# Two layers of attention scores on one core: value matmuls moved behind the first score matmul of a step, row maxima of the second layer taken from two PSUM banks by one instruction

## The chip, the cores and the metric

One core of a Trainium2 chip runs the whole kernel. The metric is the device time of one execution in microseconds (us); lower is better.

## The reference

The input x is (4, 1024, 128), with 16 heads of 8 channels. Cut to what matters here:

```
# layer 1
h      = layernorm(x)
q,k,v  = h @ Wq + bq, h @ Wk + bk, h @ Wv + bv          # (4, 16, 1024, 8)
s      = q @ k.T * 8**-0.5 + slope[h] * (i - j)          # causal: -inf above the diagonal
x      = x + layernorm(softmax(s) @ v @ Wo + bo)
# layer 2
h      = layernorm(x)
a      = softmax(q @ k.T / sqrt(8)) @ v @ Wo + bo        # not causal, no slope
u      = h + layernorm(a) * g1 + b1
x      = x + layernorm(u + layernorm(moe(u)) * g2 + b2)  # 8 experts, 2 chosen per token
```

So there are 4 x 16 score matrices of 1024 x 1024 per layer, causal in the first layer and full in the second, and each needs its row maxima before the exponentials.

## The kernel before

**Slots and steps.** The function `attend` goes through 32 slots, 16 per layer; a slot is four heads (`GH`) of one batch. `program()` writes one list of steps by hand, and each engine runs through this same list and does its own part of it, in that order. The kinds of step that matter:

- `a`: scores with queries on the partitions, only to find row maxima. TensorE writes a chunk of up to 512 columns into a PSUM bank (L388; on the causal diagonal two mask matmuls follow, L393) and VectorE takes the maximum of each row (`tensor_reduce`, L589). The a steps of a slot run one and two slots ahead of its exponentials.
- `m`: VectorE joins and splits the maxima (L598, L601, L603), after the last a of a slot. `mtr`: TensorE transposes them (L399) into a bank, VectorE copies that out (L609), and SyncE puts it into rows of the query operand `fq` by DMA.
- `b`: scores with keys on the partitions and the maxima already subtracted. TensorE writes 128x512 into one of three banks (`B_BANKS`, L411), ScalarE takes the exponential into `probs` (L474). The k-th b waits until the exponential of b number k-3 is done. Four b's, one per head, make a quad.
- `pv`: value matmuls of one quad, four heads by column groups, all into one bank (L424). `oev`: ScalarE reads this bank out at the end of half a slot (L479).
- Row steps: the work on token rows between the layers, spread over the slots by `row_steps()`: `project` (L433), `turn` (L439), `values_mm` (L443), `q` and `k` (L233 to L235), `logits` and `rank` on TensorE, each written into one bank that VectorE reads out (`y`, `turned`, `values`, `q_out`, `k_out`, `gate`, `pos`); GpSimd and SyncE do the rest.

**The inner loop.** A slot of the second layer has 16 inner steps, one of the first has 12. In inner step i the order is: the first b of quad i+3, half of the a's, the second b, the other a's, the last two b's, then `m` or `mtr` where they are due, then pv of quad i+1 (and `oev`), then the row steps. In the second layer 64 a's of one head and 512 columns fall on 16 inner steps, so about four on each (five in one of them, three in that of `mtr`). `m` is due in inner step 8 of 16 and `mtr` in step 9, behind its a's; in the first layer in steps 4 and 5 of 12.

**The ring of banks.** a, `mtr` and the TensorE row steps take the four banks `a_bank` in turn, each step one bank; `bank_free` makes TensorE wait for the reader of the step that is four places back in this ring.

**Which rows of the array.** A score matmul contracts 64 partitions, two heads, and so works in the lower or the upper half of the array (`rows_`, by head // 2). b runs through heads 0, 2, 1, 3 (`B_HEADS`), a too.

TensorE's, VectorE's, ScalarE's and GpSimd's waits are all on counts in program order, so an instruction that waits holds everything behind it on its engine.

Of the kernel before, what the change touches and what calls it, by code (L numbers as in the profile page):

```python
# [19 lines left out]
F32 = mybir.dt.float32  # L20
# [6 lines left out]
P = 128  # L27
# [13 lines left out]
HALF = 512  # L41
# [10 lines left out]
    return [start * start ** i for i in range(H)]  # L52


A_BANKS = 4
B_BANKS = 3
PROBS = 4
LOADS = 16 * 3 * GH
# [16 lines left out]
class Plan:  # L75


    def __init__(self, causal):
        self.causal = causal

        self.chunks = []
        for qt in range(TB):
            for kh in range(2):
                n = min(HALF, (qt + 1) * P - kh * HALF) if causal else HALF
                if n <= 0:
                    continue
                per = 2 if n <= HALF // 2 else 1
                for j in (0, 2) if per == 2 else (0, 2, 1, 3):
                    self.chunks.append((qt, kh, list(range(j, j + per)), n))

# [12 lines left out]
        self.mt_step = self.a_steps  # L103


PLANS = (Plan(True), Plan(False))


def plan_of(s):
    return PLANS[s // S]  # L110
# [62 lines left out]
def program():  # L173
# [10 lines left out]
    for s in range(SLOTS):  # L184
        p = plan_of(s)
        if s + 3 < SLOTS:
            out.append(("load", s + 3, 0))
        if s + 1 < SLOTS:
            out.append(("stage", s + 1, 0))
        weights = [4 - (i == p.mt_step) - .5 * (i == p.m_step) for i in range(p.nq)]  # L190
        for i in range(p.nq):
            early = i < p.a_steps
            part = range(p.a_steps) if early else range(p.a_steps, p.nq)
            target = s + 1 if early else s + 2
            ass = []
# [24 lines left out]

# [17 lines left out]
def attend(nc, loaded, query, key, rests, tokens, sums, by_head, dens, inverses, inverse_rows, ident, half_ident,  # L238
# [3 lines left out]
    with ExitStack() as ctx:  # L242
# [6 lines left out]
        def bank(name):  # L249
            return ctx.enter_context(nc.psum_tensor(f"at_{name}", [P, HALF], F32))  # L250
# [8 lines left out]
        a_bank = [bank(f"a{i}") for i in range(A_BANKS)]  # L259
        b_bank = [bank(f"b{i}") for i in range(B_BANKS)]  # L260
        pv_bank = bank("pv")

# [27 lines left out]
        for what, s, n in steps:  # L290
# [6 lines left out]
        ring = [step for step in steps if step[0] in RING]  # L297
        place = {step: k for k, step in enumerate(ring)}
# [10 lines left out]
        def done(eng, semaphore, kind, s, n, per=1):  # L309

            if (s, n) in number.get(kind, {}):
                eng.wait_ge(semaphore, per * number[kind][s, n])
# [20 lines left out]
            return qh, kt, q0, (qh + 1) * HALF - q0  # L333

        def bank_of(step):
            return a_bank[place[step] % A_BANKS]

        def block_of(x, n):
            return x[:, n * HQ:(n + 1) * HQ, :]
# [16 lines left out]
        def _(pe):  # L356
            def bank_free(step):

                if place[step] < A_BANKS:
                    return  # L360
                what, s, n = ring[place[step] - A_BANKS]
                if what == "a":
                    done(pe, a_read, "a", s, n)
                elif what == "mtr":
                    done(pe, m_read, "mtr", s, n)
                else:
                    reader = dict(project="y", turn="turned", values_mm="values", q="q_out", k="k_out", logits="gate",
                                  rank="pos")[what]
                    after(pe, reader, n)

            for step in steps:
                what, s, n = step
# [3 lines left out]
                if what == "a":  # L376
# [7 lines left out]
                    k = len(heads)  # L384
                    scores = misc[:, 0:k * w].rearrange("p (k w) -> p k w", k=k)
                    rows_ = slice(PAIR * (heads[0] // 2), PAIR * (heads[0] // 2 + 1))
                    first = heads[0] % 2
                    mm = pe.matmul(scores, fq[g][rows_, qt * P:(qt + 1) * P],  # L388
                                   km[g][rows_, first:first + k, kh * HALF:kh * HALF + w],
                                   start=True, stop=not diagonal)  # L390
                    if diagonal:
                        for i in range(2):
                            mm = pe.matmul(scores[:, :, w - P:w], half_ident[rows_, i, :],  # L393
                                           half_mask[rows_, i, None, :].broadcast_to([PAIR, k, P]),
                                           start=False, stop=(i == 1))
# [90 lines left out]
        def _(dve):  # L486
# [91 lines left out]
            for step in steps:  # L578
                what, s, n = step
                if what == "a":  # L580
                    qt, kh, heads, w = plan_of(s).chunks[n]
                    done(dve, a_made, "a", s, n)
                    if n == 0:
                        if s == 0:
                            dve.wait_ge(init, 5)
                        if s >= 1:
                            dve.wait_ge(m_step, 2 * s - 1)
                    k = len(heads)
                    dve.tensor_reduce(mx[:, kh, qt, heads[0]:heads[0] + k],  # L589
                                      bank_of(step)[:, 0:k * w].rearrange("p (k w) -> p k w", k=k),  # L590
                                      AX.X, ALU.max).then_inc(a_read, 1)
# [1289 lines left out]
```

## Time and profile before

| | |
|---|---|
| time, median of 3 runs | 1684.19 us (1681.83 to 1684.7) |
| profiled execution | 1682.8 us, span 1681.1 us |
| TensorE matmul busy | 1424.7 us (85%) |
| VectorE busy | 1296.1 us (77%) |
| ScalarE busy | 1097.2 us (65%) |
| GpSimd busy | 536.7 us (32%) |
| mean granted TensorE clock | 0.915 of full speed |

The span is time from the first to the last instruction. TensorE matmuls are pipelined, so that its busy share says little about how near it is to its peak. Slots of the first layer end at about 618 us in the trace, those of the second at 1352 us; behind that lies the expert part, which the change doesn't touch.

### The profile page before, as it was taken

The page shows a single profiled execution, that of the slowest core. Times are in us where ns is not written, and L with a number is a line of the kernel's source. Part 1 is how long each engine was busy: PE and PEld are TensorE (multiplying, and loading weights), DVE is VectorE, ACT ScalarE, POOL GpSimd, SP SyncE. Part 2 cuts the span into 40 slices and gives each one's busy share as a digit, 9 for nine tenths or more (in the row PEclk, how much of TensorE's full clock was granted, in tenths as well). Part 3 has the DMA queues.
Part 4 walks back from the last instruction along what each step waited for, and adds up shares of the span by engine and source line. Part 5 has one row for each costly group of instructions (what it writes and reads, how often), then busy time and mean ns, then how long its engine had stood idle before and what let it go on. Part 6 is the DMA issues. An engine that isn't in the chain of part 4 may idle for free. (4 is left out here: it accounts for less than half of the span.)

```text
span 1681.1 us, 27511 instructions
## 1 busy us (share of the span) xinstructions
PE 1424.7 (85%) x9143; PEld 712.0 (42%) x9143; DVE 1296.1 (77%) x2638; ACT 1097.2 (65%) x2256; POOL 536.7 (32%) x624
## 2 busy tenths in 40 slices
PE   3389999999999999999999999999999831999400
PEld 3145555555555443443344333433343221788300
DVE  4378888889888989999999999999998023655355
ACT  4036677677676557778777787778777820999444
POOL 5114544534525322340122312323141406000274
PEclk9569999999999989999999999999999965999855
DMA  6402241322322222133221122102210124788322
GB/s 168 145 28 73 84 133 50 112 81 65 102 89 72 74 71 66 43 90 91 69 65 53 52 64 78 54 32 75 61 46 33 57 78 131 224 247 248 110 63 69
DMA packets 105822, 148.96 MB, mean 89 GB/s; under 512 B 13236, under 2 KB 63164, under 8 KB 105680
## 3 DMA queue, kind: packets, MB, share of 16 engines
q1 hardware_dynamic: 100348, 138.18, 28.0%
q0 software_dynamic: 4096, 8.40, 1.7%
q8 instruction: 73, 1.20, 0.3%
q10 hardware_dynamic: 1236, 0.62, 0.2%
q14 instruction: 69, 0.57, 0.1%
HBM read 78.70 MB, written 67.13 MB: 87 GB/s over the span
## 5 line engine op out<-in xcount | busy, mean ns | idle before, releaser
L474 ACT ACTIVATE at_probs<-at_b 128x512 f32<-128x512 f32 (+3 forms) x1792 | 866.3, 557 | 380.8 <-PE at_b L411 376.2
L589 DVE TENSOR_REDUCE at_mx<-at_a 128x1 f32<-128x512 f32 (+3 forms) x1664 | 992.0, 661 | 89.5 <-PE at_a L393 28.3
L411 PE MATMUL at_b<-fq,km 64*128 64x512 f32 (+3 forms) x1792 | 669.1, 439 | 16.7 <-ACT at_probs L474 13.3
L388 PE MATMUL at_a<-km,fq 64*128 64x512 f32 (+2 forms) x1664 | 549.9, 453 | 46.3 <-DMA fq<-rest 35.2
L411 PEld LDWEIGHTS at_b<-fq,km 64*128 64x128 f32 x1792 | 295.9, 187 | 405.0 <-ACT at_probs L474 340.5
L424 PE MATMUL at_pv<-at_probs,at_vst 128*32 128x512 f32 (+3 forms) x3584 | 442.0, 566 | 0.0
L388 PEld LDWEIGHTS at_a<-km,fq 64*128 64x128 f32 x1664 | 273.8, 191 | 146.2 <-DVE at_mx L589 82.9
L747 POOL TENSOR_SCALAR_AFFINE_SELECT at_probs<-at_probs 128x512 f32<-128x512 f32 x128 | 81.5, 636 | 284.0 <-ACT at_probs L474 283.1
L1653 POOL DMA_INDIRECT t_got<-expert_out,t_out_pos x64 | 63.5, 993 | 171.4 <-issue 171.4
L424 PEld LDWEIGHTS at_pv<-at_probs,at_vst 128*32 128x32 f32 x3584 | 71.0, 108 | 104.2 <-issue 49.2
L393 PE MATMUL at_a<-half_mask,half_ident 64*128 64x128 bf16 (+1 forms) x768 | 108.7, 251 | 0.0
L1566 DVE TENSOR_TENSOR t_hid_lo<-t_hid,t_hid_hi 128x512 fp32r<-128x512 f32 x92 | 61.3, 686 | 60.5 <-ACT t_hid_hi L1419 60.5
L1414 ACT ACTIVATE t_hid<-t_bank_h,t_bias 128x512 f32<-128x512 f32 x92 | 63.0, 687 | 2.7 <-PE t_bank_h L235 2.6
L752 POOL DMA_INDIRECT expert_rows<-kept_u,route_pos x48 | 46.7, 974 | 36.5 <-DVE route_pos L873 23.5
L1419 ACT ACTIVATE t_hid_hi<-t_hid 128x512 fp32r<-128x512 f32 x92 | 55.5, 635 | 0.0
L393 PEld LDWEIGHTS at_a<-half_mask,half_ident 64*128 64x128 bf16 x768 | 43.2, 100 | 25.6 <-issue 17.4
L1577 DVE SCALAR_TENSOR_TENSOR t_z<-t_got,route_weight,t_weighed 128x128 f32<-128x128 f32 x32 | 9.1, 346 | 47.4 <-ACT t_weighed L1428 47.4
L637 POOL TENSOR_TENSOR at_rstd<-at_mean_var,pow_cols 128x4 f32<-128x4 f32 x26 | 5.3, 203 | 124.9 <-DVE at_mean_var L501 124.9
L479 ACT ACTIVATE at_osb<-at_pv 128x512 f32<-128x512 f32 x64 | 39.4, 615 | 6.2 <-PE at_pv L424 1.9
L741 POOL COPY at_vst<-tokens 128x256 f32<-128x256 f32 x32 | 12.7, 397 | 95.3 <-PE at_pv L424 95.0
L637 POOL TENSOR_TENSOR at_turned_hi<-at_t,pow_cols 128x512 fp32r<-128x512 f32 x18 | 18.7, 1041 | 69.4 <-DVE at_t L532 69.4
L233 PE MATMUL t_bank_h<-t_x_t_hi,t_w 128*128 128x512 f32 x92 | 37.0, 402 | 3.1 <-issue 1.6
(237 smaller groups left out, 1254.2 us busy)
## 6 DMA issues: line engine op xcount, KB each, us to landing
t_w<-w_parts SPq DMA_DIRECT2D x46, 512.0 KB, 4.4
sums<-at_osb SPq DMA_DIRECT2D x64, 256.0 KB, 2.0
fq<-query SPq DMA_DIRECT2D x128, 96.0 KB
km<-key SPq DMA_DIRECT2D x128, 96.0 KB
w_parts<-at_parts SPq DMA_DIRECT2D x16, 512.0 KB, 3.0
query<-at_q_hi SPq DMA_DIRECT2D x24, 256.0 KB, 3.1
key<-at_k_hi SPq DMA_DIRECT2D x24, 256.0 KB, 3.7
t_x_tok<-expert_rows SPq DMA_DIRECT2D x23, 256.0 KB, 4.8
```

Of the source, the lines that this page charges most:

```text
L388: mm = pe.matmul(scores, fq[g][rows_, qt * P:(qt + 1) * P], km[g][rows_, first:first + k, kh * HALF:kh * HALF + w], start=True, stop=not d ...
L393: mm = pe.matmul(scores[:, :, w - P:w], half_ident[rows_, i, :], half_mask[rows_, i, None, :].broadcast_to([PAIR, k, P]), start=False, sto ...
L411: pe.matmul(b_bank[k % B_BANKS][:, 0:w], km[g][rows_, j % 2, kt * P:(kt + 1) * P], fq[g][rows_, q0:q0 + w], start=True, stop=True).then_in ...
L424: mm = pe.matmul(pv_bank[HW * j:HW * (j + 1), HALF - w:HALF], vst[s % 2][:, kt, j, :], probs[n % PROBS][:, j, 0:w], start=(kt == 0), stop= ...
L474: act.activation(probs[t % PROBS][:, j, 0:w], b_bank[k % B_BANKS][:, 0:w], ACT.Exp).then_inc(exp_done, 1)
L589: dve.tensor_reduce(mx[:, kh, qt, heads[0]:heads[0] + k], bank_of(step)[:, 0:k * w].rearrange("p (k w) -> p k w", k=k), AX.X, ALU.max).the ...
L747: pool.affine_select(block_, block_, [[0, GH], [1, P]], ALU.is_ge, 0.0, base=0, channel_multiplier=-1).then_inc(masked, 1)
L752: pool.indirect_dma_start(out=xs[:, :], out_offset=bass.IndirectOffsetOnAxis(ap=routing["pos"][:, k, t:t + 1], axis=0), in_=kept_u[:, t, : ...
L1414: op = act.activation(hid[:, f, :], h_bank[f][:, :], ACT.Gelu, bias=bias[:, n, f:f + 1])
L1419: op = act.activation(hid_hi[i][:, f, :], hid[:, f, :], ACT.Identity)
L1566: op = dve.tensor_tensor(hid_lo[i][:, f, :], hid[:, f, :], hid_hi[i][:, f, :].bitcast(F32), ALU.subtract)
L1653: pool.indirect_dma_start(out=got[i][:, k, t, :], out_offset=None, in_=ys[:, :], in_offset=bass.IndirectOffsetOnAxis(ap=out_pos[:, k, n * ...
```

## The change

1. In `program()` pv of quad i+1 and its `oev` come right behind the first b of inner step i; `m`, `mtr` and the row steps stay at the end of the step. The a's now lie between the second, third and fourth b.
2. In the second layer a chunk is a pair of heads, (0, 2) or (1, 3), in two neighbouring banks. TensorE writes both (in the other order in every second chunk, so that the array halves alternate), then one `tensor_reduce` of 128 x 2 x 512 reads both. A slot has 32 such chunks in place of 64, two in each inner step.
3. The ring now counts places: a pair must start at an even place, so behind a single bank's use one place is skipped. `bank_free` waits for the last users of all places that a step takes.

```diff
-                for j in (0, 2) if per == 2 else (0, 2, 1, 3):
-                    self.chunks.append((qt, kh, list(range(j, j + per)), n))
+                if paired:
+                    self.chunks += [(qt, kh, (tuple(range(j, j + per)), tuple(range(j + 2, j + 2 + per))), n)
+                                    for j in range(0, 2, per)]
...
-PLANS = (Plan(True), Plan(False))
+PLANS = (Plan(True, False), Plan(False, True))
...
-            out += bs[:1] + ass[:half] + bs[1:2] + ass[half:] + bs[2:]
+            out += bs[:1]
+            at, q = (s, i + 1) if i + 1 < p.nq else (s + 1, 0)
+            if at < SLOTS:
+                out.append(("pv", at, q))
+                if q in plan_of(at).half_end:
+                    out.append(("oev", at, plan_of(at).half_end.index(q)))
+            out += bs[1:2] + ass[:half] + bs[2:3] + ass[half:] + bs[3:]
             if s + 1 < SLOTS:
                 if i == p.m_step:
                     out.append(("m", s + 1, 0))
                 if i == p.mt_step:
                     out.append(("mtr", s + 1, 0))
-            at, q = (s, i + 1) if i + 1 < p.nq else (s + 1, 0)
-            if at < SLOTS:
-                out.append(("pv", at, q))
-                if q in plan_of(at).half_end:
-                    out.append(("oev", at, plan_of(at).half_end.index(q)))
             out += rows.get((s, i), [])
...
+        place, users_before, users = {}, {}, [None] * (2 * A_PAIRS)
+        spot = 0
+        for step in steps:
+            if step[0] in RING:
+                width = len(plan_of(step[1]).chunks[step[2]][2]) if step[0] == "a" else 1
+                spot += spot % width
+                place[step] = spot % len(users)
+                taken = range(place[step], place[step] + width)
+                users_before[step] = [u for k, u in enumerate(users) if k in taken and u is not None]
+                for k in taken:
+                    users[k] = step
+                spot += width
...
-                if place[step] < A_BANKS:
-                    return
-                what, s, n = ring[place[step] - A_BANKS]
-                if what == "a":
-                    done(pe, a_read, "a", s, n)
+                for what, s, n in users_before[step]:
+                    if what == "a":
+                        done(pe, a_read, "a", s, n)
...
+                    parts = list(enumerate(heads))
+                    for at, js in parts[::-1] if n % 2 else parts:
+                        k = len(js)
+                        bank_ = misc if len(heads) == 1 else pair_with(step)[:, at, :]
...
+                    elif k == 1:
+                        dve.tensor_reduce(mx[:, kh, qt, j:j + 3:2], pair_with(step)[:, :, 0:w], AX.X,
+                                          ALU.max).then_inc(a_read, 1)
```

## Rows read from the trace of the kernel before

**Rows 1.** Windows: span, busy us (instructions) of PE, PEld, DVE, ACT, POOL, clock, DMA.
```profile
300.00:400.00 100.00, 98.76 (x809) 51.63 (x805) 86.29 (x178) 71.02 (x164) 43.54 (x56) 1.00 0.31 93
570.00:618.00 48.00, 45.76 (x228) 20.34 (x229) 43.33 (x82) 22.51 (x51) 15.12 (x19) 0.86 0.12 30
1100.00:1200.00 100.00, 98.34 (x587) 38.14 (x590) 95.64 (x176) 78.43 (x153) 22.91 (x31) 1.00 0.21 65
1320.00:1345.00 25.00, 20.67 (x119) 6.00 (x111) 0.00 (x0) 20.05 (x40) 11.50 (x12) 1.00 0.17 61
```

**Rows 2.** Waits from 800 to 1300 us: total, times, longest.
```profile
PEld at_b L411 <- ACT at_probs L474: 166.7, 276, 1.7
```

**Rows 3.** Timeline, last slot, where no a is left: start, length, engine, instructions.
```profile
1323.21 0.73 PE L411 MATMUL at_b<-fq,km 64*128 64x512 f32 x3
1323.74 2.07 ACT L474 ACTIVATE at_probs<-at_b 128x512 f32<-128x512 f32 x4 [0.53 <-PE at_b L411]
1324.39 0.49 PE L411 MATMUL at_b<-fq,km 64*128 64x512 f32 x1 [0.45 <-ACT at_probs L474]
1324.81 1.06 PE L424 MATMUL at_pv<-at_probs,at_vst 128*32 128x512 f32 x8
1325.81 0.73 PE L411 MATMUL at_b<-fq,km 64*128 64x512 f32 x3
```

**Rows 4.** Timeline, second layer with its a's, three stretches.
```profile
1002.38 0.50 PE L411 MATMUL at_b<-fq,km 64*128 64x512 f32 x1
...
1003.56 0.18 PEld L411 LDWEIGHTS at_b<-fq,km 64*128 64x128 f32 x1 [0.29 <-ACT at_probs L474]
...
1004.98 0.50 PE L411 MATMUL at_b<-fq,km 64*128 64x512 f32 x1
...
1006.40 7.36 DVE L589 TENSOR_REDUCE at_mx<-at_a 128x1 f32<-128x512 f32 x12
...
1013.21 0.50 PE L411 MATMUL at_b<-fq,km 64*128 64x512 f32 x1
...
1013.98 2.48 DVE L589 TENSOR_REDUCE at_mx<-at_a 128x1 f32<-128x512 f32 x4 [0.21 <-PE at_a L388]
```

**Rows 5.** Groups by form, 60 to 700 us: busy us, mean ns, idle before.
```profile
L589 DVE TENSOR_REDUCE at_mx<-at_a 128x1 f32<-128x512 f32 x579 | 359.7, 680 | 27.1 <-PE at_a L393 14.0 <-PE at_a L388 11.2
...
L589 DVE TENSOR_REDUCE at_mx<-at_a 128x1 f32<-128x384 f32 x128 | 64.2, 548 | 10.4 <-PE at_a L393 10.2
```

**Rows 6.** Timeline, logits with a project behind pv, and a turn behind pv.
```profile
1061.16 0.27 PE L233 MATMUL at_a<-gw_hi,at_turned_hi 128*128 128x8 f32 x1
...
1063.59 0.50 PE L411 MATMUL at_b<-fq,km 64*128 64x512 f32 x1
...
1086.19 0.66 PE L439 MATMUL at_a<-ident,kept_u 128*128 128x128 f32 x4
1086.78 0.49 PE L411 MATMUL at_b<-fq,km 64*128 64x512 f32 x1
```

**Rows 7.** Timeline, an inner step with mtr, from its first b.
```profile
1066.19 0.50 PE L411 MATMUL at_b<-fq,km 64*128 64x512 f32 x1
...
1066.87 0.19 DVE L598 TENSOR_TENSOR at_mfull<-at_mx 128x32 f32<-128x32 f32 x1
...
1067.32 0.21 DVE L603 TENSOR_TENSOR at_m_parts<-at_mfull,at_m_parts 128x32 fp32r<-128x32 f32 x1
...
1067.81 0.33 PE L399 MATMUL at_a<-ident,at_m_parts 128*128 128x128 f32 x1
...
1068.07 1.06 PE L424 MATMUL at_pv<-at_probs,at_vst 128*32 128x512 f32 x8
```

**Rows 8.** Timeline, the value matmuls around the step with five a's.
```profile
1074.32 1.06 PE L424 MATMUL at_pv<-at_probs,at_vst 128*32 128x512 f32 x8
...
1077.29 1.07 PE L424 MATMUL at_pv<-at_probs,at_vst 128*32 128x512 f32 x8
```

More of the change, by code:

```diff
@@ L52, in slopes @@
     return [start * start ** i for i in range(H)]
-A_BANKS = 4
+A_PAIRS = 2
 B_BANKS = 3
@@ L75, with __init__ @@
 class Plan:
-    def __init__(self, causal):
+    def __init__(self, causal, paired):
         self.causal = causal
@@ L87, in __init__ @@
                 per = 2 if n <= HALF // 2 else 1
-                for j in (0, 2) if per == 2 else (0, 2, 1, 3):
-                    self.chunks.append((qt, kh, list(range(j, j + per)), n))
+                if paired:
+                    self.chunks += [(qt, kh, (tuple(range(j, j + per)), tuple(range(j + 2, j + 2 + per))), n)
+                                    for j in range(0, 2, per)]
+                else:
+                    self.chunks += [(qt, kh, (tuple(range(j, j + per)),), n)
+                                    for j in ((0, 2) if per == 2 else (0, 2, 1, 3))]
         self.quads = []
@@ L258, in attend @@
         osb = sb("osb", [P, 2, HALF])
-        a_bank = [bank(f"a{i}") for i in range(A_BANKS)]
+        a_pair = [ctx.enter_context(nc.psum_tensor(f"at_a{i}", [P, 2, HALF], F32)) for i in range(A_PAIRS)]
         b_bank = [bank(f"b{i}") for i in range(B_BANKS)]
@@ L296, in attend @@
                 series[s, n] = len(series) + 1
-        ring = [step for step in steps if step[0] in RING]
-        place = {step: k for k, step in enumerate(ring)}
+        place, users_before, users = {}, {}, [None] * (2 * A_PAIRS)
[10 more added lines that the diff above has]
+                spot += width
         row_order = [(what,) + n for what, s, n in steps if what in ENGINE_OF]
@@ L335, in bank_of, with pair_with @@
         def bank_of(step):
-            return a_bank[place[step] % A_BANKS]
+            return pair_with(step)[:, place[step] % 2, :]
+        def pair_with(step):
+            return a_pair[place[step] // 2]
         def block_of(x, n):
@@ L357, in bank_free @@
             def bank_free(step):
-                if place[step] < A_BANKS:
-                    return
-                what, s, n = ring[place[step] - A_BANKS]
-                if what == "a":
-                    done(pe, a_read, "a", s, n)
[L364 to L369, printed above, removed]
+                for what, s, n in users_before[step]:
+                    if what == "a":
+                        done(pe, a_read, "a", s, n)
+                    elif what == "mtr":
+                        done(pe, m_read, "mtr", s, n)
+                    else:
+                        reader = dict(project="y", turn="turned", values_mm="values", q="q_out", k="k_out", logits="gate",
+                                      rank="pos")[what]
+                        after(pe, reader, n)
             for step in steps:
@@ L382, in _ @@
                     diagonal = plan_of(s).causal and kh * HALF + w == (qt + 1) * P
[L384 to L395, printed above, removed]
+                    parts = list(enumerate(heads))
+                    for at, js in parts[::-1] if n % 2 else parts:
+                        k = len(js)
+                        bank_ = misc if len(heads) == 1 else pair_with(step)[:, at, :]
+                        scores = bank_[:, 0:k * w].rearrange("p (k w) -> p k w", k=k)
+                        rows_ = slice(PAIR * (js[0] // 2), PAIR * (js[0] // 2 + 1))
+                        first = js[0] % 2
+                        mm = pe.matmul(scores, fq[g][rows_, qt * P:(qt + 1) * P],
+                                       km[g][rows_, first:first + k, kh * HALF:kh * HALF + w],
+                                       start=True, stop=not diagonal)
+                        if diagonal:
+                            for i in range(2):
+                                mm = pe.matmul(scores[:, :, w - P:w], half_ident[rows_, i, :],
+                                               half_mask[rows_, i, None, :].broadcast_to([PAIR, k, P]),
+                                               start=False, stop=(i == 1))
                     mm.then_inc(a_made, 1)
@@ L587, in _ @@
                             dve.wait_ge(m_step, 2 * s - 1)
[L588 to L591, printed above, removed]
+                    k, j = len(heads[0]), heads[0][0]
+                    if len(heads) == 1:
+                        dve.tensor_reduce(mx[:, kh, qt, j:j + k],
+                                          bank_of(step)[:, 0:k * w].rearrange("p (k w) -> p k w", k=k),
+                                          AX.X, ALU.max).then_inc(a_read, 1)
+                    elif k == 1:
+                        dve.tensor_reduce(mx[:, kh, qt, j:j + 3:2], pair_with(step)[:, :, 0:w], AX.X,
+                                          ALU.max).then_inc(a_read, 1)
+                    else:
+                        dve.tensor_reduce(mx[:, kh, qt, :].rearrange("p (h k) -> p h k", k=k),
+                                          pair_with(step)[:, :, 0:k * w].rearrange("p h (k w) -> p h k w", k=k), AX.X,
+                                          ALU.max).then_inc(a_read, 1)
                 elif what == "m":
```

## Prediction, made before the changed kernel was run

> **What bounds the kernel now.** I read the windows first [rows 1]. In the second layer TensorE shows 98 us of work in 100, VectorE 96, ScalarE 78. That looks as if VectorE, next to full, set the pace. The last of these windows contradicts it: there no a is left, VectorE does nothing, and yet, as the timeline shows, the loop has not become faster. So I looked for the period of the inner step.
>
> In the last slot the first b of a step starts at 1323.21 and that of the next at 1325.81: 2.60 us [rows 3]. With four a's and their reductions the same distance is 1004.98 - 1002.38 = 2.60 us [rows 4]. Taking away the whole of VectorE's work changes nothing, so it is not the bound of an ordinary step. What is, can be followed in the same rows: first b at 1323.21; ScalarE starts on it at 1323.74 (0.53 later); the fourth b must have the bank of the first and starts at 1324.39, 1.18 behind the first, after an exponential of some 0.6 and a semaphore's delay; the value matmuls start 0.42 later, at 1324.81; and the next first b is 1.00 behind them. 0.53 + 0.65 + 0.42 + 1.00 = 2.60. In the chain of waits the same wait is the largest, 166.7 us in 500 [rows 2]. With a's running, TensorE is held for only 0.29 us of a step at that place [rows 4], because the a's fill the rest; still it is held.
>
> The second thing that a step can be held by is VectorE's backlog. Four reductions take 4 x 0.607 = 2.43 us when they run without a gap (12 in 7.36 us: 7.36 less one length of 0.68, by 11 [rows 4, 5]), so 0.17 us of a step is spare, and where VectorE has other work it lags and TensorE waits for a bank.
>
> **Part 1, the order of b and pv.** Written as a line, the new order looks different. The loop is a cycle, though, and I start both at pv:
>
> before: pv, b, a's, b, a's, b, b, pv
> after: pv, b, a's, b, a's, b, b, pv
>
> They are the same. Only the names have moved: the b behind pv used to be the first of its quad and is now the second. B_BANKS is 3 in both, so the fourth b of a burst still waits for the exponential of the first one of that burst, and pv stands behind it. The chain is 2.60 us as before. I take this part at 0 for an ordinary step; the chance that it does release the chain is a rival below. pv of a quad now runs one burst earlier with respect to its exponentials and, in the first layer, to GpSimd's diagonal masks. Almost a full cycle is left between them; I take 0. `oev` stands between the same instructions of ScalarE's cycle as before: 0. Behind an earlier pv the buffer of probabilities comes free earlier, and nothing waits for it.
>
> What does move in the cycle are `mtr` and TensorE's row steps. Before, a row step stood behind pv, and `mtr` between the fourth b and pv. Now both stand between the third b and the fourth, so the fourth b and pv queue behind them, and what they wait for counts in full.
>
> **Part 2, one reduction for two banks.** The trace has no reduction of 1024 columns. From 384 to 512 columns it goes from 548 to 680 ns [rows 5], 1.03 ns a column, so one of 1024 should take 0.68 + 0.53 = 1.21 us, and without a gap 1.21 - 0.07 = 1.14 against 2 x 0.607 = 1.21 for two. A pair saves 0.07, and 512 pairs save 38 us of VectorE's time. The lower bound is no saving, the upper one 2 x 0.68 - 1.21 = 0.15 a pair, if instructions didn't overlap at all.
>
> The Trainium skill (VectorE: DVE Perf Modes, The DRAIN you can't avoid) says that the next instruction does not start until the pipe is empty. By that rule a pair saves the 0.15; the trace differs, since 12 reductions of 0.68 us fit in 7.36 us, and the measurement decides.
>
> Little of the 38 us can come out of the time, because an ordinary step isn't VectorE's. What can: the inner step with five a's takes 1077.29 - 1074.32 = 2.97 us [rows 8] and becomes one of two pairs, -0.37, in about 12 slots (this row stands for them): -4. In the stretch 570 to 618 us the first layer's last slot has 64 a's of the second layer in 12 inner steps and VectorE is at 43 of 48 us [rows 1]; there 32 pairs save 2.4 us. Backlogs behind the statistics and the routing work shrink a little: -3. Together -9; bounds 0 and -20.
>
> **Part 3, the ring.** This is where I expect the loss. In an inner step of the second layer the pairs X and Y now fill all four banks. A single use at the end of the step (`mtr` or a row step) takes the first bank of X, and TensorE must wait until VectorE has read all of X. Before, it waited for the use four places back, an a that was long read.
>
> When is X read? Count from the b behind pv. The reduction of the first a's starts 1013.98 - 1013.21 = 0.77 later [rows 4], and that is about when both a's of X are there. So X is read from 0.77 to 1.98, and a single can start at 2.03 with a semaphore's 0.05. Then the fourth b follows, which on an ordinary step starts at 1.18.
>
> *Row steps in the second layer.* A turn behind pv costs its own time, 1086.78 - 1086.19 = 0.59, and logits with project 1063.59 - 1061.16 = 2.43 [rows 6]. That remains. On top of it comes 2.03 - 1.18 = 0.85, since the fourth b starts that much later than it otherwise would. By the tables of row steps such a place occurs 26 times while pairs are running (10 from the last rows of the first layer, 16 for the second's three batches, the logits and project of one step sharing a pair). 26 x 0.85 = 22. Bounds: 0 if X was read in time, 1.2 each (31) if VectorE lags by 0.35 more.
>
> *mtr in the second layer.* m starts at 1066.87, 0.68 behind the first b, ends at about 1067.53 (1.34), and `mtr` runs at 1067.81 (1.62), pv at 1068.07, 1.88 behind the b where 1.60 is usual: it costs 0.28 now [rows 7]. In the new order X of this step stands behind m on VectorE and ahead of `mtr` on TensorE, by the same rule. So `mtr` waits for m and then for 1.21 us of X: reductions end about 0.13 sooner, m ends at 1.20, X is read until 2.42, `mtr` starts at 2.47, the fourth b 0.27 later at 2.74, against 1.18: it costs 1.56. That is +1.28 in each of 16 slots (those whose a's belong to the second layer at that time): +20. Bounds 0.9 and 1.8 each, 14 to 29. What waits behind: b, pv, and through them ScalarE, which has nothing to do for over a microsecond, and VectorE after Y.
>
> *First layer.* The a's are single and the ring as before. A row step there costs one change of array shape more, since the sequence b, row step, b, pv has one more than b, pv, row step, b. The third b is through by about 0.9 (the fourth's 0.29 of waiting ends at 1.18 [rows 4]) and a change of shape takes 0.42 (from b to pv [rows 3]), so a row step starts at about 1.3, where the fourth b wants to start at 1.18: +0.12, and more where VectorE lags, as it often does there (86 of 100 us [rows 1]). I take 0.2 for 46 row steps, +9, and 0.13 for 14 `mtr`, +2; bounds 0 and 30.
>
> The Trainium skill (TensorEngine Tiling (Array Packing), Key Properties) has it that changing the tiling mode drains TensorE. The trace agrees so far: 0.42 us from a lone b to pv. By the rule alone the first layer would be put at 46 x 0.12 = 6 us.
>
> **Sum.** +22 + 20 + 11 - 9 = +44 us. On the profiled execution's 1682.8 this is 1727; the median lies 1.4 above that, so 1729.
>
> **Rivals.** (a) *VectorE was the pace after all*, and the pairs free it: 512 x 0.07 = 38 us less, 1646. For it: 96 of 100 us busy. Against: 2.60 us without any reduction. It decides only if most steps wait for banks rather than for the exponential. By the skill's page on VectorE it would be 512 x 0.15 = 75 us, 1609; I give this 0.02 of the chance.
> (b) *The new order breaks the chain*: the wait of 0.29 us in a step goes, 256 x 0.29 = 74 us, 1610. For it: pv could cover the exponential. Against: the cycle above, with the fourth b ahead of pv in both.
> (c) *The singles' wait is hidden*, because VectorE is ahead: then parts 2 and 3 leave +2 to +11 - 9, that is 1680 to 1690. Against: X can't be read before it is written, 0.77 behind the burst's start.
> (d) *The waits add up with lag*: upper bounds, 31 + 29 + 30 - 5 = +85, 1769.
>
> **Chances.** Forecast (slower by some 17 to 68) 0.66; (d) 0.08; (c) 0.12; (a) and (b) 0.14 together. A difference of 0.2%, 3.4 us, is about what a measurement of this kernel can tell from none. Of (c) I count 0.04 within it, 0.06 slower and 0.02 faster: slower 0.66 + 0.08 + 0.06 = 0.80, same 0.04, faster 0.02 + 0.14 = 0.16. For 8 times in 10 the range is 1690 to 1752; it leaves out (a), (b) and the end of (d). If the forecast's mechanism holds, its own range is 1701 to 1752.
>
> **What the profile after should show.** The period of an ordinary step still 2.60 us, with the fourth b held by the exponential of the first of its burst. Reductions of 128x2 from 1024 columns of 1.21 us, 512 of them, and VectorE's idle time larger, not smaller. TensorE waiting for the reduction (L589's successor) ahead of `mtr` and the row steps of the second layer, about 40 times at 0.8 to 1.3 us. Steps with `mtr` at 4.1 to 4.2 us, with a turn at 4.0. The first layer's length within 20 us of what it was. Wrong would be: an ordinary step clearly under 2.60 (then the cycle argument fails), or singles that start at once (then part 3 fails).

## The result, and the profile after

The changed kernel takes 1728.6 us (median of 4 runs, 1724.93 to 1733.97) against 1683.4 for the kernel before beside it (4 runs): 1.0271 times as long, 95% interval 1.0242 to 1.0301. The forecast was 1729 (1690 to 1752). Its profiled execution took 1724.93 us, with a span of 1723.2 us and a mean granted clock of 0.908.

The windows come first again; the columns are those of [rows 1]. From the second on, the stretches lie later than those of before, as the kernel itself does, and the second is longer.

```profile
300.00:400.00 100.00, 97.47 (x800) 49.62 (x797) 84.49 (x170) 70.28 (x162) 42.34 (x55) 1.00 0.32 96
575.00:640.00 65.00, 52.76 (x310) 23.11 (x308) 53.04 (x59) 31.80 (x72) 21.42 (x26) 0.84 0.22 67
1110.00:1210.00 100.00, 95.01 (x550) 35.57 (x550) 83.06 (x96) 70.29 (x136) 26.46 (x34) 0.93 0.19 55
1360.00:1385.00 25.00, 20.38 (x114) 6.13 (x112) 0.00 (x0) 20.06 (x40) 13.97 (x15) 1.00 0.18 66
```

In the second layer VectorE went from 96 us in 100 to 83, and ScalarE, whose work is the same, from 78 to 70. The second number says that the stretch got slower; the first, that VectorE's amount of work does not set its pace: it has more idle time than before. TensorE can still wait for a single reduction, and the timelines below show that it does. In the last slot, where no a is left, 25 us hold the same 40 exponentials as before. The profile's page, in its groups of instructions over the whole span, shows VectorE's cheaper work (name, form, count, then busy us, mean ns, idle before):

```profile
L613 DVE TENSOR_REDUCE at_mx<-at_a 128x2 f32<-128x1024 f32 x512 | 600.0, 1217 | 109.6 <-PE at_a L407 109.4
L609 DVE TENSOR_REDUCE at_mx<-at_a 128x1 f32<-128x512 f32 (+3 forms) x640 | 359.6, 628 | 101.2 <-PE at_a L412 44.6
```

A pair is 1217 ns long; the estimate was 1.21 us.

**Where the time went.** `oev`, the read-out of the value bank, marks the end of each slot. Slots are counted from 0, so slot 15 is the first layer's last.

| us | before | after | change | my terms |
|---|---|---|---|---|
| slots 0 to 14, ends at | 570.2 | 581.5 | +11.3 | +11 |
| slot 15 | 48.1 | 52.7 | +4.6 | -2.4 |
| second layer, 16 slots | 732.9 | 760.4 | +27.5 | +22 +20 -6.6 |
| behind it, to the span's end | 329.9 | 328.6 | -1.3 | 0 |
| span | 1681.1 | 1723.2 | +42.1 | +44 |

In the text below a single is a use of one bank by `mtr` or a row step, and X is the first pair of an inner step.

**An ordinary step** of the changed kernel, one without a single, in the timeline:

```profile
1008.47 0.49 PE L430 MATMUL at_b<-fq,km 64*128 64x512 f32 x1
...
1009.10 0.21 PEld L407 LDWEIGHTS at_a<-km,fq 64*128 64x128 f32 x2 [0.34 <-DVE at_mx L613]
...
1009.24 2.36 DVE L613 TENSOR_REDUCE at_mx<-at_a 128x2 f32<-128x1024 f32 x2 [0.25 <-PE at_a L407]
...
1009.65 0.18 PEld L430 LDWEIGHTS at_b<-fq,km 64*128 64x128 f32 x1 [0.25 <-ACT at_probs L493]
...
1010.07 1.07 PE L443 MATMUL at_pv<-at_probs,at_vst 128*32 128x512 f32 x8
1011.07 0.50 PE L430 MATMUL at_b<-fq,km 64*128 64x512 f32 x1
```

From the b behind pv to the next one: 1011.07 - 1008.47 = 2.60 us. The last b of the burst starts 1.18 behind the first, released by the exponential, pv 0.42 later, the next b 1.00 later. These are the three terms of [rows 3]. New is that VectorE is idle for 0.25 us of the step and that an a waits 0.34 for the reduction of the pair ahead. Neither lengthens the step.

**The step with `mtr`**:

```profile
1001.77 0.50 PE L430 MATMUL at_b<-fq,km 64*128 64x512 f32 x1
...
1002.33 0.19 DVE L625 TENSOR_TENSOR at_mfull<-at_mx 128x32 f32<-128x32 f32 x1
...
1002.91 2.35 DVE L613 TENSOR_REDUCE at_mx<-at_a 128x2 f32<-128x1024 f32 x2
...
1004.18 0.33 PE L418 MATMUL at_a<-ident,at_m_parts 128*128 128x128 f32 x1 [1.04 <-DVE at_mx L613]
1004.44 0.50 PE L430 MATMUL at_b<-fq,km 64*128 64x512 f32 x1
1004.87 1.06 PE L443 MATMUL at_pv<-at_probs,at_vst 128*32 128x512 f32 x8
1004.97 0.60 ACT L493 ACTIVATE at_probs<-at_b 128x512 f32<-128x512 f32 x1 [1.09 <-PE at_b L430]
1005.86 0.50 PE L430 MATMUL at_b<-fq,km 64*128 64x512 f32 x1
```

m is short (0.19), but VectorE then reads pair X from 1002.91, and `mtr` wants X's first bank. The trace names the reduction as releaser, 1.04 us. `mtr` starts 2.41 behind the first b, the last b 2.67 and pv 3.10; the prediction had 2.47 and 2.74. ScalarE meanwhile stands idle for 1.09 us. The step takes 1005.86 - 1001.77 = 4.09 us.

That is the undisturbed step. In five of the second layer's 15 steps with `mtr` VectorE has other work between m and X, and the step takes 4.7 to 5.25 us. In three of them it is the statistics of a row step:

```profile
1096.32 0.19 DVE L625 TENSOR_TENSOR at_mfull<-at_mx 128x32 f32<-128x32 f32 x1
...
1096.90 0.86 DVE L517 BATCH_NORM_STATS2 at_stats<-at_y 128x6 f32<-128x128 f32 x4
...
1098.09 2.32 DVE L613 TENSOR_REDUCE at_mx<-at_a 128x2 f32<-128x1024 f32 x2
...
1099.34 0.33 PE L418 MATMUL at_a<-ident,at_m_parts 128*128 128x128 f32 x1 [2.21 <-DVE at_mx L613]
```

X is read from 1098.09 here, some 1.2 us later, and `mtr` waits 2.21 in place of 1.04. With single banks in the same order (e1 below) the steps that hold nothing but `mtr` all take 2.93 to 2.95 us. So a pair makes `mtr` pay for what else VectorE does ahead of it.

**The step with a turn**:

```profile
1115.37 0.50 PE L430 MATMUL at_b<-fq,km 64*128 64x512 f32 x1
...
1116.14 2.36 DVE L613 TENSOR_REDUCE at_mx<-at_a 128x2 f32<-128x1024 f32 x2 [0.35 <-PE at_a L407]
...
1117.42 0.66 PE L458 MATMUL at_a<-ident,kept_u 128*128 128x128 f32 x4 [0.79 <-DVE at_mx L613]
1118.01 0.50 PE L430 MATMUL at_b<-fq,km 64*128 64x512 f32 x1
1118.44 1.06 PE L443 MATMUL at_pv<-at_probs,at_vst 128*32 128x512 f32 x8
```

X is read from 0.77 behind the first b (predicted 0.77), the turn starts at 2.05 (2.03). The waits from 640 to 1395 us count how often this happens (total, times, longest):

```profile
DVE at_mx L613 <- PE at_a L407: 98.0, 189, 3.5
...
PEld at_a L418 <- DVE at_mx L613: 26.2, 15, 2.6
...
PEld at_a L238 <- DVE at_mx L613: 9.4, 8, 1.3
...
PEld at_a L458 <- DVE at_mx L613: 9.2, 8, 1.2
...
PEld at_a L452 <- DVE at_mx L613: 5.6, 5, 1.1
```

L238 is the helper of q, k and logits, L458 the turn, L452 the project. With two more lines of two waits each (`values_mm` and rank) single uses of a bank wait for a pair's reduction 40 times. The first line says that in the same stretch VectorE waited 98 us for TensorE: what it saves turns into idle time.

**Account of the second layer.** I took every step from pv to pv, and added up what it lies over 2.60 us, by what it holds.

| steps, us over 2.60 each | before | after | change in all |
|---|---|---|---|
| turn (8) | 0.59 | 1.46 | +7.0 |
| project (5) | 1.49 | 1.96 | +2.3 |
| logits (3) | 1.44 | 2.50 | +3.2 |
| logits and project (3) | 2.43 | 3.30 | +2.6 |
| other row steps (8, then 7) | 0.91 | 1.49 | +3.1 |
| with `mtr` (15) | 0.80 | 1.81 | +15.2 |

That is +18 and +15, 33 in all. Added up in the same way, the steps without singles lie 27.5 us over before and 19.2 after, so 8 less. The 3 us that are then still missing to the slots' +27.5 are about one step, which the count has more after than before (254 and 253).

### The profile page after: what moved, and what is told of

Same layout as the page of the kernel before. It is cut to its first block and busy times, and to the rows that moved or that the text cites. A ratio compares the mean times of both kernels' runs of the same rounds, so it can differ in the third digit from the quotient of the medians.

```text
span 1723.2 us, 27495 instructions
## 1 busy us (share of the span) xinstructions
PE 1422.6 (83%) x9143; PEld 684.9 (40%) x9143; DVE 1255.3 (73%) x2126; ACT 1106.2 (64%) x2256; POOL 537.6 (31%) x624
## 5 line engine op out<-in xcount | busy, mean ns | idle before, releaser
L493 ACT ACTIVATE at_probs<-at_b 128x512 f32<-128x512 f32 (+3 forms) x1792 | 876.0, 556 | 416.1 <-PE at_b L430 410.3
L613 DVE TENSOR_REDUCE at_mx<-at_a 128x2 f32<-128x1024 f32 x512 | 600.0, 1217 | 109.6 <-PE at_a L407 109.4
L430 PE MATMUL at_b<-fq,km 64*128 64x512 f32 (+3 forms) x1792 | 658.5, 437 | 14.2 <-ACT at_probs L493 9.6
L407 PE MATMUL at_a<-km,fq 64*128 64x512 f32 (+2 forms) x1664 | 507.8, 463 | 53.4 <-DMA fq<-rest 35.9
L430 PEld LDWEIGHTS at_b<-fq,km 64*128 64x128 f32 x1792 | 299.6, 189 | 457.0 <-ACT at_probs L493 402.2
L443 PE MATMUL at_pv<-at_probs,at_vst 128*32 128x512 f32 (+3 forms) x3584 | 449.1, 574 | 0.4 <-ACT at_probs L493 0.4
L609 DVE TENSOR_REDUCE at_mx<-at_a 128x1 f32<-128x512 f32 (+3 forms) x640 | 359.6, 628 | 101.2 <-PE at_a L412 44.6
L407 PEld LDWEIGHTS at_a<-km,fq 64*128 64x128 f32 x1664 | 235.7, 192 | 151.0 <-DVE at_mx L613 84.0
```

The costliest lines, as they stand in the source:

```text
L407: mm = pe.matmul(scores, fq[g][rows_, qt * P:(qt + 1) * P], km[g][rows_, first:first + k, kh * HALF:kh * HALF + w], start=True, stop=not d ...
L430: pe.matmul(b_bank[k % B_BANKS][:, 0:w], km[g][rows_, j % 2, kt * P:(kt + 1) * P], fq[g][rows_, q0:q0 + w], start=True, stop=True).then_in ...
L443: mm = pe.matmul(pv_bank[HW * j:HW * (j + 1), HALF - w:HALF], vst[s % 2][:, kt, j, :], probs[n % PROBS][:, j, 0:w], start=(kt == 0), stop= ...
L493: act.activation(probs[t % PROBS][:, j, 0:w], b_bank[k % B_BANKS][:, 0:w], ACT.Exp).then_inc(exp_done, 1)
L609: dve.tensor_reduce(mx[:, kh, qt, j:j + k], bank_of(step)[:, 0:k * w].rearrange("p (k w) -> p k w", k=k), AX.X, ALU.max).then_inc(a_read, 1)
L613: dve.tensor_reduce(mx[:, kh, qt, j:j + 3:2], pair_with(step)[:, :, 0:w], AX.X, ALU.max).then_inc(a_read, 1)
```

## The experiments

Every kernel was timed beside the kernel before (1681.9 to 1682.7 us). Edits are against the changed kernel where nothing else is said.

### The parts by themselves

**e1_order**: the new order with single banks in the second layer too.

```diff
-PLANS = (Plan(True, False), Plan(False, True))
+PLANS = (Plan(True, False), Plan(False, False))
```

> The new order alone: pv behind the first b, but both layers with one a per bank and one reduction each. My theory (the cycle of b's and pv is the same, only mtr and the row steps have moved in front of the fourth b; the wait for a whole pair is what makes them dear in the second layer): ordinary steps 2.60 us, the first layer up to 582 us as in the changed kernel (570 before), mtr steps of the second layer at about 3.3 instead of 4.08, row steps there about 0.15 above before; in all 1683 + 11 + 6 + 4 = 1704 (1692 to 1712). Rival 1, the order is the whole loss: 1729. Rival 2, the pairs are the whole loss: 1683, and the first layer ends where it did before.

Measured: 1693.6 us, 1.0079 (1.0055 to 1.0103), less than expected but inside the range. Slots 0 to 14 end at 579.9, slot 15 takes 54.2, the second layer 726.8: 6 us less than before. So the first layer's whole loss comes from the order, and the second layer's is nothing that the order does alone. (The 6 us less are no gain of the order that is shown: in the kernel before, four steps are lengthened by some 7 us by a meeting that this kernel happens not to have; more on it below.) In the timeline `mtr` waits only for m here, and the last b follows 1.52 behind the first, in place of 2.67:

```profile
1077.05 0.49 PE L430 MATMUL at_b<-fq,km 64*128 64x512 f32 x1
...
1078.34 0.30 PE L418 MATMUL at_a<-ident,at_m_parts 128*128 128x128 f32 x1 [0.33 <-DVE at_m_parts L630]
1078.57 0.50 PE L430 MATMUL at_b<-fq,km 64*128 64x512 f32 x1
1078.99 1.07 PE L443 MATMUL at_pv<-at_probs,at_vst 128*32 128x512 f32 x8
```

**e2_pairs**: pairs with the old order. **e3_pairs_late**: the same, with `mtr` behind pv as well.

```diff
e2
-            out += bs[:1]
-            at, q = (s, i + 1) if i + 1 < p.nq else (s + 1, 0)
-            if at < SLOTS:
-                out.append(("pv", at, q))
...
-            out += bs[1:2] + ass[:half] + bs[2:3] + ass[half:] + bs[3:]
+            out += bs[:1] + ass[:half] + bs[1:2] + ass[half:] + bs[2:]
...
+            at, q = (s, i + 1) if i + 1 < p.nq else (s + 1, 0)
+            if at < SLOTS:
+                out.append(("pv", at, q))
...
             out += rows.get((s, i), [])
e3, against e2
-                if i == p.mt_step:
-                    out.append(("mtr", s + 1, 0))
...
+            if s + 1 < SLOTS and i == p.mt_step:
+                out.append(("mtr", s + 1, 0))
             out += rows.get((s, i), [])
```

> The pairs alone: the order of before (pv and the row steps behind the fourth b, mtr between the fourth b and pv). My theory: row steps find the pair read by the time pv is over and cost nothing more than before; mtr still waits for m and a reduction of 1024 columns, about 0.9 us in 16 slots = +14; the last slot of the first layer, where four pairs go through two places in a step, +4; steps with five a's gone, -4, backlogs -3: 1694 (1684 to 1702). Rival 1 (the order is the whole loss): 1683 or less. Rival 2 (the pairs are the whole loss): 1729. Rival 3 (fewer VectorE instructions pay): 1683 - 38 = 1645.

> As the pairs alone, but mtr is put behind pv, where it finds its bank read. My theory: the 14 us of e2_pairs go away, mtr steps at about 2.9 us: 1680 (1672 to 1690). Rival: if the wait ahead of mtr is hidden or is not for the pair, no difference to e2_pairs.

Measured: e2 1686.5 us, 1.0032 (1.0022 to 1.0043), inside its range but under the 1694 expected; e3 1678.9, 0.9975 (0.9963 to 0.9987), as expected. From e2 to e3 it gains 7.6 us, though, not the 14 that I had put on `mtr`'s wait: the shortest steps with `mtr` fell from 3.65 to 3.15 us, not to 2.9. The order alone costs 11 us, the pairs alone 4, both 46 (1.0271 of 1682): some 30 us belong to neither, only to their meeting. With pairs and the row steps behind pv the step with a turn takes 3.19 us as before, and one with a project 3.69, where single banks took 4.19: in such steps VectorE did lag, and pairs give 0.5 back.

**e5_mtr_late**: the kernel before, with `mtr` behind pv and nothing else. **e6_two_reduces**: e3, with each pair read by two reductions of 512.

```diff
-                        dve.tensor_reduce(mx[:, kh, qt, j:j + 3:2], pair_with(step)[:, :, 0:w], AX.X,
+                        dve.tensor_reduce(mx[:, kh, qt, j:j + 1], pair_with(step)[:, 0, 0:w], AX.X, ALU.max)
+                        dve.tensor_reduce(mx[:, kh, qt, j + 2:j + 3], pair_with(step)[:, 1, 0:w], AX.X,
                                           ALU.max).then_inc(a_read, 1)
```

> The kernel before with mtr behind pv and nothing else (single banks, one reduction each). It tells whether the gain of e3_pairs_late (0.25% below before) comes from the pairs or from the place of mtr. My theory: with single banks mtr is held by m alone and costs about 0.28 on either side of pv, so 1682 within 3, and the gain belongs to the pairs. Rival: the place of mtr is what gains, 1678.

> e3_pairs_late (pairs, old order, mtr behind pv), but each pair is read by two reductions of 512 columns, both behind the wait for both banks. If one instruction in place of two is what lets the pairs gain, VectorE's time goes up by 0.07 a pair and some backlogs with it: 1679 + 4 to 8 = 1683 to 1687. If the even spread of two pairs per step is the gain, no change, 1679. If VectorE set the pace, + 38.

Measured: e5 1678.2 us, 0.9976 (0.9966 to 0.9985), more of a gain than I expected and as much as e3's; e6 1691.9, 1.0055 (1.0040 to 1.0069), slower than expected. So e3's gain is `mtr`'s place; the pairs add nothing to it. Of the pairs e6 shows both sides: taking the banks two at a time, with everything that goes with it in the order of the a's, costs 1691.9 - 1678.2 = 13.7 us, and one instruction in place of two gives 1691.9 - 1678.9 = 13.0 back.

### Is the exponential's chain what sets 2.60 us?

The prediction rests on it, and so far only rows spoke for it. **e4_four_b** and **e7_two_b** change the kernel before in its split of the seven banks, **e8_longer_exp** lengthens in it one exponential of four.

```diff
e4
-A_BANKS = 4
-B_BANKS = 3
+A_BANKS = 3
+B_BANKS = 4
e7
-A_BANKS = 4
-B_BANKS = 3
+A_BANKS = 5
+B_BANKS = 2
e8
-                    act.activation(probs[t % PROBS][:, j, 0:w], b_bank[k % B_BANKS][:, 0:w], ACT.Exp).then_inc(exp_done, 1)
+                    lot = P if n % GH == 0 else w
+                    for at in range(0, w, lot):
+                        mm = act.activation(probs[t % PROBS][:, j, at:at + lot], b_bank[k % B_BANKS][:, at:at + lot],
+                                            ACT.Exp)
+                    mm.then_inc(exp_done, 1)
```

> The kernel before with one bank moved from the a ring to the b ring (3 and 4 in place of 4 and 3), nothing else. The fourth b of a burst then needn't wait for the exponential of the first. If that chain sets the step of 2.60 us, as I said, ordinary steps fall to VectorE's four reductions, 2.43 to 2.5 us, and the whole by 0.1 to 0.17 in some 250 steps of the second layer and by 5 to 20 us in the first: 1630 to 1655. Rival 1, TensorE or VectorE sets the pace: 1683 within 5. Rival 2, three banks are too few for the a's and VectorE is starved: slower than 1690.

> The kernel before with one bank moved from the b ring to the a ring (5 and 2). The chain that I hold for the pace then gets longer: the fourth b of a burst waits for the exponential of the second, 0.53 + 0.48 + 0.6 + 0.05 = 1.66 behind the first, pv at 2.08, the next burst at 3.08 us in place of 2.60. 252 steps of the second layer by 0.48 = +121, the first layer by 0.2 to 0.45 in 190 steps, +60: 1830 to 1880. Rival (VectorE's pace, TensorE waiting for a's banks): five banks help it, 1683 or less.

> The kernel before, but the exponential of the first b of each quad is made in pieces of 128 columns (four for 512), the same values. Its result comes 3 x 0.21 + 0.28 = 0.9 us after its start and not 0.6; ScalarE's load goes from 2.06 to about 2.4 us a step, still under 2.60. If the wait of the fourth b for that exponential sets the step, ordinary steps go from 2.60 to 2.90: +75 in the second layer, +15 to +40 in the first: 1770 to 1800. If VectorE or TensorE sets it, no change up to 0.29 us of waiting that it may hide: 1683 to 1690.

Measured: e4 1848.5 us, 1.1017 (1.0967 to 1.1067), far off my expectation; it is the second rival that came true. Its timeline shows another wait in the place of the chain's:

```profile
1207.27 0.50 PE L411 MATMUL at_b<-fq,km 64*128 64x512 f32 x1
...
1208.78 0.18 PEld L388 LDWEIGHTS at_a<-km,fq 64*128 64x128 f32 x1 [0.98 <-DVE at_mx L589]
1208.78 0.72 PE L411 MATMUL at_b<-fq,km 64*128 64x512 f32 x2
1209.44 1.06 PE L424 MATMUL at_pv<-at_probs,at_vst 128*32 128x512 f32 x8
1210.43 0.49 PE L411 MATMUL at_b<-fq,km 64*128 64x512 f32 x1
```

With three banks an a waits 0.98 us for its reduction, and the last b's and pv stand behind it on TensorE: 3.16 us a step. So this run says nothing on the chain; it says that the a's had no bank to spare. What it did show is the mechanism of the change's loss, from the other side.

e7 took 1852.1 us, 1.1015 (1.0980 to 1.1051). With two banks the third b, not the fourth, waits for the first exponential, and 3.08 us a step were expected:

```profile
1100.75 0.50 PE L411 MATMUL at_b<-fq,km 64*128 64x512 f32 x1
1101.29 2.27 ACT L474 ACTIVATE at_probs<-at_b 128x512 f32<-128x512 f32 x4 [0.83 <-PE at_b L411]
...
1102.43 0.18 PEld L411 LDWEIGHTS at_b<-fq,km 64*128 64x128 f32 x1 [0.31 <-ACT at_probs L474]
...
1102.86 1.06 PE L424 MATMUL at_pv<-at_probs,at_vst 128*32 128x512 f32 x8
1103.86 0.50 PE L411 MATMUL at_b<-fq,km 64*128 64x512 f32 x1
```

1103.86 - 1100.75 = 3.11, median 3.10, with more banks for the a's than before. e8 took 1738.7 us, 1.0325 (1.0304 to 1.0346), under the 1770 to 1800 that I expected: its pieces follow each other more closely than I had taken, and the last b gets its bank 0.19 later:

```profile
1043.44 0.50 PE L411 MATMUL at_b<-fq,km 64*128 64x512 f32 x1
...
1044.81 0.18 PEld L411 LDWEIGHTS at_b<-fq,km 64*128 64x128 f32 x1 [0.27 <-ACT at_probs L476]
...
1045.23 1.06 PE L424 MATMUL at_pv<-at_probs,at_vst 128*32 128x512 f32 x8
1046.23 0.49 PE L411 MATMUL at_b<-fq,km 64*128 64x512 f32 x1
```

1044.81 - 1043.44 = 1.37 in place of 1.18, and the step takes 2.79 in place of 2.60. A delay of one exponential comes out of the step one to one. With e7 that shows the chain in the kernel before; the miss was in the size of the edit.

### Is it where the singles stand?

Pairs with the old place of pv (e2), but with the single uses moved ahead of the fourth b, as they stand in the changed kernel's cycle: **e9_front_all** `mtr` and row steps, **e10_front_rows** only the row steps, **e11_front_mtr** only `mtr`.

```diff
e9, against e2
-            out += bs[:1] + ass[:half] + bs[1:2] + ass[half:] + bs[2:]
+            out += bs[:1] + ass[:half] + bs[1:2] + ass[half:] + bs[2:3]
...
+            out += rows.get((s, i), [])
+            out += bs[3:]
...
-            out += rows.get((s, i), [])
```

> Pairs, and pv left behind the fourth b of its step as before; only mtr and the row steps are put between the third b and the fourth. If the cycle argument holds (moving pv behind the first b of the next step is only a renaming, and the whole effect of the new order is where mtr and the row steps stand), this is as slow as the changed kernel: 1728 within 6. Rival: the earlier pv itself costs something (the exponentials and masks that it waits for, another pairing of widths in the first layer): then this is nearer to e2_pairs, 1687 to 1715.

> As e9_front_all, but mtr stands between the fourth b and pv as before; only the row steps are in front of the fourth b. My theory: e2_pairs' 1687 + 0.85 x 26 = 22 in the second layer + about 8 in the first and 4 in its last slot: 1720 (1710 to 1726). Rival (mtr is the larger part): 1700.

> As e9_front_all, but the row steps stand behind pv as before; only mtr is in front of the fourth b. In e2_pairs an mtr step takes 3.65 us and in the changed kernel 4.08, so 16 x 0.43 = +7, and +2 in the first layer: 1695 (1690 to 1702). With e10_front_rows the two parts should add up to e9_front_all.

Measured: e9 1731.0 us, 1.0291 (1.0277 to 1.0306); e10 1724.0, 1.0235 (1.0210 to 1.0261), 4 over what I expected; e11 1701.3, 1.0111 (1.0097 to 1.0126), 6 over; all three are inside their ranges. Against e2 the row steps' place costs 37.5 us, `mtr`'s 14.7, both 44.5. The two parts make 52 and not 44.5, so they do not simply add up, as I had expected with e11; why is not shown. The steps have the lengths of the changed kernel: with a turn 4.07 us in e10 and 3.19 in e11, with `mtr`, where nothing else delays it, 3.65 in e10 and 4.09 in e11. e9's total is the changed kernel's to 3 us, but not by the same parts: up to slot 14 the changed kernel lost 7 us more, and e9 13 more in the second layer (773.8), where three of its m's met work of GpSimd and the steps with `mtr` average 5.0 us against 4.4. This agreement is partly chance.

**e12_rename** does the reverse: the changed kernel, with `mtr` and the row steps held back until behind the next step's pv. Only the names in the cycle are then left of the change of order.

```diff
+    held = []
...
-            out += bs[1:2] + ass[:half] + bs[2:3] + ass[half:] + bs[3:]
+            out += held + bs[1:2] + ass[:half] + bs[2:3] + ass[half:] + bs[3:]
...
-                if i == p.mt_step:
-                    out.append(("mtr", s + 1, 0))
-            out += rows.get((s, i), [])
+            held = [("mtr", s + 1, 0)] if s + 1 < SLOTS and i == p.mt_step else []
+            held += rows.get((s, i), [])
```

> The changed kernel (pv behind the first b of its step, pairs in the second layer), but mtr and the row steps of a step are held back until behind the pv of the next one, so that in the cycle from pv to pv they stand where e3_pairs_late has them. If the new order is only a renaming apart from them, it is as fast as e3_pairs_late: 1679 within 4, turn steps of 3.19 us and project steps of 3.69. Rival: the earlier pv is itself what costs (in the first layer the changed kernel lost 7 us more than e9_front_all, and 6 us of waiting for GpSimd stand there): 1686 or more.

Measured: 1683.2 us, 1.0006 (0.9991 to 1.0021), just outside the 1679 within 4 that I expected and under the rival's 1686. Of the 46 us some 45 are gone, with pv still behind the first b and pairs still in use. All three parts come back: slots 0 to 14 end at 571.1, slot 15 takes 48.1 and the second layer 733.5. Against e3, which has the same cycle, 4 us are left, which I had put at 0. They may be pv's earlier place with respect to its exponentials and to GpSimd, or in part one more m that meets work of GpSimd (four here, three in e3); no run separates these.

## Why the prediction was right

**The total** is partly luck. It came out within 1 us, but slot 15 took 7 us more than its term and the second layer 8 less. What was right is the mechanism, part by part:

**The cycle.** Right, and shown by runs: e12 moves pv and changes nothing that could be told from 1683; e7 and e8 move the period by what the chain says.

**Part 2.** Four pairs without a gap take 4.62 us (line below), (4.62 - 1.22)/3 = 1.13 each, where two single reductions take 1.21: the 0.07 was right, and so was that most of it does not come out of the time: the steps without singles gave 8 us back, where some 7 were forecast for the second layer. The prediction quotes the drain rule without its exception, which stands in the same section: the Trainium skill (VectorE: DVE Perf Modes, The DRAIN you can't avoid) also says that a next operation that is not held starts earlier. The overlap of 0.08 us here (1.217 - 1.133) agrees with the exception and not with the rule alone. By itself the part came to +4 where I had -9, since with the old order `mtr` already waits for a pair (undisturbed steps with it 3.65 in e2, 2.87 before). I had priced that wait only in the new order. In the sum it makes no difference, as `mtr`'s term holds it.

**Part 3, second layer.** The mechanism came out, and in undisturbed steps its times to 0.07 us. 22 for the row steps were 18: in the five steps with a project alone the pairs give back 0.4 to 0.5 of the 0.9, and the three with rank grew by 0.2 only. 20 for `mtr` were 15, the balance of two things that I hadn't seen. The five steps with other VectorE work between m and X, shown above, cost 5 us more than undisturbed ones. On the other side, before, in four of the steps with `mtr` m met a GpSimd instruction, and the step took 4.4 to 4.9 us. In the changed kernel no m does so:

```profile
1016.26 1.28 POOL L637 TENSOR_TENSOR at_heads_t<-at_num_in,at_inv_in 128x512 f32<-128x512 f32 x1 [13.80 <-DMA at_inv_in<-inverses]
...
1016.50 1.10 DVE L598 TENSOR_TENSOR at_mfull<-at_mx 128x32 f32<-128x32 f32 x1
1017.63 1.18 DVE L601 CAST at_m_parts<-at_mfull 128x32 fp32r<-128x32 f32 x1
```

That is the kernel before: 1.10 us in place of 0.19, and the cast behind it took 1.18 in place of 0.19, beside the next GpSimd instruction. The Trainium skill (SBUF, two separate sides) says that VectorE and GpSimd share a pair of ports which one of them holds for a whole instruction, a VectorE operation with two inputs in SBUF among them. The trace agrees: m ended at 1017.60, right behind the GpSimd instruction's end at 1017.54. Such meetings are chance in this schedule, as far as one profiled execution of each kernel shows: three in e2, e3, e5, e6, e9 and e11, four in e10 and e12, none in the changed kernel and in e1. Four steps of some 4.6 us in place of 2.87 are 7 us, by which the change looks better than it is.

**The first layer.** +11.3 up to slot 14 against +11, but not by my terms: a step with `mtr` alone there takes 2.87 us in both kernels, not 0.13 more. That the sum agrees is luck. Instead TensorE now waits for GpSimd, from 110 to 570 us:

```profile
PE at_a L238 <- POOL at_turned_lo L664: 4.6, 7, 0.8
...
PE at_a L452 <- POOL at_heads_t L664: 1.2, 3, 0.4
```

Before there is no such wait, nor in e9. A row step's place now comes one pv sooner, ahead of its input. 5.8 us of the 11.3 stand in these two lines. Nearly all of the 11.3 go with the place of the singles, since e12 ends slot 14 only 0.9 us later than the kernel before; e9, with the singles in front but pv in its old place, 4.3 later. Whether these 4.3 are the change of array shape, no run here takes apart.

**Slot 15** is a term with the wrong sign: -2.4 forecast, +4.6 measured. I had read VectorE's 43 of 48 us [rows 1] as its being the bound. The timeline of the changed kernel there:

```profile
593.58 3.49 DVE L613 TENSOR_REDUCE at_mx<-at_a 128x2 f32<-128x1024 f32 x3 [1.30 <-PE at_a L407]
...
594.95 0.79 PE L407 MATMUL at_a<-km,fq 64*128 64x512 f32 x2 [0.98 <-DVE at_mx L613]
...
597.95 4.62 DVE L613 TENSOR_REDUCE at_mx<-at_a 128x2 f32<-128x1024 f32 x4 [0.88 <-PE at_a L407]
```

Three pairs or more go through two places in one step, and each engine waits for the other in turn. The mean granted clock of the window is 0.84, where the kernel before had 0.89 in the same one. But single banks in the new order lose 6 there (e1), pairs in the old order 2.6 (e2) and with `mtr` behind pv nothing (e3, 47.3): here too it is mostly the order. And of the order it is again the place of the singles, since e12 takes 48.1, as before. What failed in this term is that it priced only VectorE's saving and no wait of TensorE for a bank.

**Rivals.** (a) and (b) are out by the windows and the step of 2.60. (c), the hidden wait, by 40 waits that the trace names (its terms, +2 to +11 - 9 on 1684, give 1677 to 1686, not the 1680 to 1690 of the prediction; the measured time is outside both). (d), with waits lengthened by VectorE's lag, would have been 1769; for the row steps they are at their undisturbed size, 1.3 us at most, but for `mtr` it holds in the five steps above, up to 2.6 us.

## What to carry to other kernels

Write an engine's order as a cycle before pricing a move: what has only changed its name costs next to nothing (e12, 4 us over e3), and what changed places with a neighbour is the edit. Making an instruction wait for two banks at a time is paid by the uses of one bank behind it in the ring, and the price is that of all that queues behind them, so put those uses behind the work that the cycle waits for, not ahead of it. The place of `mtr` alone was worth 0.24% here (e5), as much as the best version with pairs (e3, 0.25%), and both beat the two kernels.

## What the runs showed of the hardware

One reduction over two neighbouring banks, 128x2x512, takes 1217 ns, where one bank takes 680; back to back 1.13 us against 2 x 0.607. An exponential in four pieces of 128 columns frees its bank only 0.19 us later than one of 512. A VectorE operation of 0.19 us beside a GpSimd tensor operation of 1.28 took 1.10, and the cast behind it, 0.19 us alone, took 1.18.
